# Two-layer recurrent block: ones on TensorE during the first loads, the next layer's input turned inside the first layer's tail

## The reference

```python
xn = layernorm(x)
s = L0_attention(xn)     # 32 heads of 16, 8 key/value heads, softmax, output projection Wo
g = silu(L0_ffn(xn))     # Hadamard transforms, up and gate products (2048), Hadamard transform, down product
x = x + s * g
xn = layernorm(x)
s = L1_attention(xn)     # q, k, v through a causal convolution of 4 taps and SiLU; gated delta rule over
                         # 6 heads of 64; RMS norm, gate, output projection
g = silu(L1_ffn(xn))     # sign(up) and sign(down) weights, ReLU between them
x = x + s * g
```

## Time and profile before

| | us |
|---|---|
| median of 3 runs | 1447.39 (1447.01 to 1448.87) |
| profiled execution | 1447.84 |
| its span | 1445.1 |
| TensorE busy | 1352.4 |
| VectorE busy | 1074.3 |
| ScalarE busy | 722.7 |
| GpSimd busy | 519.0 |
| second layer's block starts | 741.74 |

### The profile page before, as it was taken

The page is one execution under the profiler, slowest core; times in us unless marked ns, Lnnn a source line. Parts: engine busy times, 40 slices in busy tenths (PEclk is TensorE's granted clock), DMA queues, the critical chain, the costliest instruction groups (busy, mean ns, idle before and its releaser), DMA issues. The chain is left out here.

```text
span 1445.1 us, 24309 instructions
## 1 busy us (share of the span) xinstructions
PE 1352.4 (94%) x8972; PEld 663.8 (46%) x8972; DVE 1074.3 (74%) x1874; ACT 722.7 (50%) x1277; POOL 519.0 (36%) x434
## 2 busy tenths in 40 slices
PE   5988999999999999999889999998999899998998
PEld 2332333333333333333345458554675447654485
DVE  7889887787778787888728668578677796676745
ACT  5675665556656665566555513554235332354221
POOL 3599750122102220122116522274313543155331
PEclk9999999999999999999999999999999999999989
DMA  6420000000010000102530240001400113102211
GB/s 240 158 81 3 7 8 14 28 27 4 9 34 19 14 8 22 31 13 88 206 147 6 51 88 17 30 23 34 88 23 23 46 26 73 38 8 57 40 20 44
DMA packets 79573, 68.51 MB, mean 47 GB/s; under 512 B 45952, under 2 KB 67168, under 8 KB 76896
## 3 DMA queue, kind: packets, MB, share of 16 engines
q1 hardware_dynamic: 79456, 66.96, 15.6%
HBM read 44.87 MB, written 17.87 MB: 43 GB/s over the span
## 5 line engine op out<-in xcount | busy, mean ns | idle before, releaser
L610 DVE TENSOR_REDUCE mS<-bank 128x1 f16<-128x512 f32 x512 | 328.9, 685 | 114.5 <-PE bank L1113 112.4
L925 ACT ACTIVATE probs<-bank 128x512 f16<-128x512 f32 x512 | 277.2, 595 | 163.4 <-PE bank L1120 163.1
L1167 PE MATMUL bank<-rows,both 128*128 128x512 f16 x1024 | 243.0, 380 | 0.4 <-DVE th L639 0.3
L425 POOL TENSOR_TENSOR h<-th,h 128x512 f16<-128x512 f32 x61 | 71.5, 1172 | 219.0 <-ACT h L896 219.0
L1167 PEld LDWEIGHTS bank<-rows,both 128*128 128x128 f16 x1024 | 91.3, 98 | 121.2 <-issue 15.5
L2094 PE MATMUL fbank<-rows,both 128*128 128x512 f16 x512 | 119.1, 387 | 4.7 <-ACT hid L1915 4.7
L2078 PE MATMUL abank<-rows,both 128*128 128x512 f16 (+1 forms) x480 | 114.0, 390 | 4.6 <-PEq L149 4.6
L1113 PE MATMUL bank<-qk 32*128 32x512 f16 x512 | 100.5, 387 | 15.7 <-DVE mS L610 6.5
L2110 PE MATMUL fbank<-both,hid 128*128 128x512 f16 x512 | 111.2, 379 | 0.0
L1120 PE MATMUL bank<-qv,qk 32*128 32x512 f16 x512 | 99.9, 387 | 0.0
L1181 PE MATMUL bank<-dn,h 128*128 128x512 f16 x256 | 98.7, 386 | 0.0
(11 more groups left out here) (326 smaller groups left out, 2675.4 us busy)
## 6 DMA issues: line engine op xcount, KB each, us to landing
h<-in_ug SPq DMA_DIRECT2D x8, 1024.0 KB, 5.1
lt_scratch<-big SPq DMA_DIRECT2D x16, 384.0 KB, 2.7
dn<-in_down SPq DMA_DIRECT2D x2, 2048.0 KB, 11.0
x_scratch<-th SPq DMA_DIRECT2D x16, 256.0 KB, 2.2
res<-x_scratch SPq DMA_DIRECT2D x16, 256.0 KB, 3.6
out_x<-res SPq DMA_DIRECT2D x16, 256.0 KB, 2.0
both<-in_w SPq DMA_DIRECT2D x2, 1548.0 KB, 10.3
t_scratch<-tok SPq DMA_DIRECT2D x8, 384.0 KB, 3.5
```

The lines of the kernel that those rows point to most:

```text
L425: pool.tensor_tensor(h16(ft, 1), row32, h16(ft, 0), ALU.subtract).then_inc(S["row_lo"], 1)
L610: v.tensor_reduce(mS[:, u % 2, qt, 32 * j + DH:32 * j + DH + 1], SA[n % 2][:, :], AX.X, ALU.max).then_inc(S["max_done"], 1)
L925: a.activation(probs[:, n % (2 * G), :], SB[n % 2][:, :], ACT.Exp, scale=float(DH) ** -0.5).then_inc(S["p_ready"], 1)
L1167: mm = pe.matmul(GB[n % 2][:, :], w[:, kt, col:col + P], xnb(b, kt), start=r == 0, stop=r == 2 * KT - 1)
```

## The change

- TensorE no longer begins with the wait for the constants. It waits for `allone` and multiplies it with itself `WARM = 22` times (f32, 128x128 by 128 columns) into the bank `OB`, which nothing reads; then it waits for the constants as before.
- The second output projection of each batch moves from step 19 to step 20 (`OUT_STEP`), and with it its gate, residual and store. The residual inputs get a list of their own, `XRES_STEP = (17, 20, 24, 25)`: the third and the fourth are asked for at steps 24 and 25, not 28 and 35.
- `turn_next` moves from behind the last step to step 20 of the tail, ahead of that step's output projection. ScalarE's four `next_evict` move to the same step, behind its third sign.
- After the last step TensorE runs `project_next`: the 24 matmuls of the second layer's first `ba` and `pre_tile(0)`, into the banks that `layer1` expects them in. For this the eight banks are allocated once for both layers. In `layer1`, batch 0, these two tiles are left out and only their semaphore is raised.

```diff
-OUT_STEP = (17, 19, 28, 35)
+NEXT_STEP = 20
+OUT_STEP = (17, 20, 28, 35)
+XRES_STEP = (17, 20, 24, 25)
...
+WARM = 22
...
+    W["vpair"] = ctx.enter_context(nc.psum_tensor("vpair", [P, 2, 512], F32))
+    W["banks"] = [W["vpair"][:, 0], W["vpair"][:, 1]] + [ctx.enter_context(nc.psum_tensor(f"bank{i}", [P, 512], F32))[:, :] for i in range(2, 8)]
...
-                if b >= 0 and m in OUT_STEP:
-                    tt = OUT_STEP.index(m)
+                if b >= 0 and m in XRES_STEP:
+                    tt = XRES_STEP.index(m)
...
                 if t - B * BSTEPS in SIGN_AT:
                     raw_sign(SIGN_AT.index(t - B * BSTEPS))
-            for kt in range(KT):
-                next_evict(kt)
+                if t - B * BSTEPS == NEXT_STEP:
+                    for kt in range(KT):
+                        next_evict(kt)
...
         def _(pe):
+            pe.wait_ge(S["init"], 1)
+            for n in range(WARM):
+                pe.matmul(OB[:, 0:P], allone[:, :], allone[:, :], start=True, stop=True)
             pe.wait_ge(S["const_in"], 32)
...
+            def project_next():
+                pe.wait_ge(S["t_w1l"], KT)
+                pe.wait_ge(S["t_took"], KT)
+                pe.wait_ge(S["o_free"], NU)
+                for i, w in enumerate((slice(4 * KW, NW1), slice(ORDER[0] * P, ORDER[0] * P + P))):
+                    n = 0
+                    for kt in range(KT):
+                        for x, y in ((0, 0), (0, 1), (1, 0)):
+                            mm = pe.matmul(bank[3 + i][0:w.stop - w.start, :], W["w1"][:, x, kt, w], W["xT"][:, kt, y, :],
+                                           start=n == 0, stop=n == 3 * KT - 1)
+                            n += 1
+                    mm.then_inc(S["t_turn"], 1)
+                pe.wait_ge(S["t_turn"], KT + 2)
...
+                if b == B and m == NEXT_STEP:
+                    turn_next()
                 if b and m in OUT_STEP:
                     project_o((b - 1) * TT + OUT_STEP.index(m))
-            turn_next()
+            project_next()
...
-                three(bk[0:2 * LH, :], lambda i, kt: w1[:, i, kt, 4 * KW:NW1], x_half).then_inc(S["a_full"], 1)
+                if b:
+                    three(bk[0:2 * LH, :], lambda i, kt: w1[:, i, kt, 4 * KW:NW1], x_half).then_inc(S["a_full"], 1)
+                else:
+                    pe.sem_inc(S["a_full"], 1)
...
-                pre_tile(0)
+                if b:
+                    pre_tile(0)
+                else:
+                    afill("pre", 0)
+                    pe.sem_inc(S["a_full"], 1)
```

More of the change, by code:

```diff
@@ L154, in sem @@
             return ctx.enter_context(nc.semaphore(name))
-        bank = [ctx.enter_context(nc.psum_tensor(f"bank{i}", [P, 512], F32)) for i in range(8)]
+        bank = W["banks"]
         SA, SB, OB, GB, MISC = bank[0:2], bank[2:4], bank[4], bank[5:7], bank[7]
@@ L1303, in sem @@
             return ctx.enter_context(nc.semaphore(name))
-        vpair = ctx.enter_context(nc.psum_tensor("vpair", [P, 2, 512], F32))
-        vbank = [vpair[:, 0], vpair[:, 1], ctx.enter_context(nc.psum_tensor("vbank2", [P, 512], F32))]
-        abank = [ctx.enter_context(nc.psum_tensor(f"abank{i}", [P, 512], F32)) for i in range(3)]
-        fbank = [ctx.enter_context(nc.psum_tensor(f"fbank{i}", [P, 512], F32)) for i in range(2)]
+        vpair, vbank, abank, fbank = W["vpair"], W["banks"][0:3], W["banks"][3:6], W["banks"][6:8]
         ident16, cmat, rowm, blocks, hsel, onec, expo = (W[n] for n in ("ident16", "cmat", "rowm", "blocks", "hsel", "onec", "expo"))
```

## The result

The changed kernel takes **1449.78 us** (median of 20 executions, 1444.72 to 1456.46), the kernel before 1446.32 (median of 20 beside them, 1441.42 to 1448.87): 1.0028 of the time, 95% interval 1.0016 to 1.0039. It is slower by 3.5 us, where 6.0 us less had been forecast, and it lies above the range. The profiled execution takes 1449.62 us with a span of 1447.8.

What follows compares the result with a forecast made beforehand. TensorE, busy 94% of 1445.1 us, was taken as the bound, with waits or slow stretches in the first 27 us and at the seam. Terms -0.2 + 0.9 - 2.0 - 4.7 = -6.0 gave 1441.4 us, range 1437.0 to 1444.6.

Steps and rivals of the forecast that it cites:

- Ones: Kernel start: 22 added products hide before the first transposes, but scores from 22 us still start slow; -0.2 us.
- D: Kernel start: ones' weight loads and products don't overlap and the clock stays low, delaying the start; 1449.1 us, chance 0.04.
- The projection a step later: Three batches inside the loop: TensorE's q projection waits 0.3 us more for VectorE's product each time; +0.9 us.
- End of the first layer: First layer's tail: earlier loads let last signs and tanh start 1.7 us earlier, last-input wait gone; -2.0 us.
- rival B: Seam between layers: loads hold it (-0.8) and the third tile runs slow throughout (-3.7); 1443.6 us, chance 0.15.
- First tiles: Second layer's start: third tile complete 6.9 us after the block starts instead of 11.6; -4.7 us.
- Rival C: Second layer's start: VectorE's convolutions set the pace, so held tiles buy nothing; 1446.1 us, chance 0.06.
- Rival A: Seam: clock stays high, third tile comes at 4.5 us instead of 6.9; 1439.0 us, chance 0.15.

Runs made afterwards that it cites:

- short loads: Changed kernel without ones and with step 19 in the middle, its sixth to eighth raw weight loads cut to an eighth: 1431.79 us, one execution.
- filling products: Changed kernel without ones at the start and with step 19 in the middle, plus 7 products of ones ahead of the held tiles: 1444.22 us, 0.9982 of before.

## Why the prediction was wrong

- **Ones, -0.2 us.** At its place the term was right, and so was each of its steps: done at 8.6, fast projections, a pause of 4.56 us, scores where they were, -0.1 us at 260. The scores behind the pause were slow as foretold: projections 1.07 us, then the transform at 22.50 takes 2.08, and with 12 products in the pause 1.12. The rule of the Trainium skill that the prediction cites (page TensorE: Matmul & The Clock Gate, section HAM oscillation), that a long wait returns the clock to half, agrees with this. What failed is the sentence "So they cost nothing": I counted TensorE's time and left out that 88 more instructions (44 products and their weight loads) move everything fetched behind them. The runs put that at 3.0 to 7.2 us. None of my rivals had it; D foretold 1449.1, near what was measured, for another reason, records that do not overlap; that is refuted by 7.62 us for 44, so its number is luck.
- **The projection a step later, +0.9 us.** It is 3.3. The 0.3 us for the product were measured as 0.24. The step that failed is that I looked only at where the projection arrives and not at what it left: at step 19 its 1 us lay in a wait for VectorE's maxima.
- **End of the first layer, -2.0 us.** -0.5, less than my bound of -0.8, and not shown to be the change's. The step that failed is that the last signs and the last tanh start 1.7 us earlier: they start no earlier, since the eighth load landed when it had landed before, although its issue moved. That is the part of rival B on the loads. The short loads show that these loads hold the end. The working has a slip, too: its 1.7 and 0.5 us add up to 2.2, not 2.0, and TensorE's work as listed ends near 735.9, not 736.9.
- **First tiles, -4.7 us.** -3.9, near the bound (-3.7) for a third tile that is slow throughout, and -4.1 to -4.6 in four other traces. The mechanism was right: TensorE's 24 new matmuls and the turn hid as said, its pause is 3.46 us where 3.5 had been forecast, and it starts low again. The granted clock is 0.68 over 745 to 750.
- **Sum.** -0.1 + 3.3 - 0.5 - 3.9 = -1.2 us. With the three steps of 1.3 us at the shifted fetches this is +2.7, and with the half clock behind two more long waits (2 x 5.5 x 7/23 = 3.3) +6.0; with the rates of the second and the third batch, 4/5 and 1/6, it would be +8.0. The measured +3.5 lies between the first two, which says no more than that the parts are large enough. The kernel without the ones and with step 19 in the middle takes 1440.39, within the forecast's own width and 1.0 us from 1441.4. That is partly luck: it gains 5.4 us where the prediction's two terms for the seam say 6.7, and the forecast started from a median of 1447.39 of three executions, the comparison from 1445.74. The seam is worth near 5 us, less than it was taken for, and the ones and step 20 took more than that back.

Rival C (held tiles buy nothing) fell: without them the seam keeps 0.6 of its 4.3 us. Rival A did not occur in any trace; with filling products a part of it did, 1.0 us.

## What to carry to other kernels

Before an instruction is moved, ask what its old place was hiding as well as what the new one costs: a projection that sat in a wait cost 1.1 us a batch when it was moved, not the 0.3 us that were visible. Before instructions are added "for nothing" in an unrolled kernel, remember that they shift the instruction fetches of all that follows; after such an edit compare the traces stage by stage, also where nothing was edited, and test with instructions of the same number and no work. And where loads and the last consumer stand in a chain, issuing a load earlier can gain nothing: here the DMA engines were full, and the last tanh came no earlier.

## What the hardware showed unexpectedly

- One instruction packet of 16 KB among data transfers went with 1.1 to 1.4 us of delay for the engine that waited for the last of them, in 16 of 19 cases.
- A wait of TensorE of 1.4 to 1.7 us ahead of 24 products of 64x64 was followed by half clock for some 14 us in 7 of 23 cases, one of 0.7 us or less in none of 25. At 5.5 us each this could make much of the scatter between executions of one kernel, whose times go with their mean granted clock (correlation -0.95 in 35 executions); that it is these stretches was not tested.
- 44 f32 records of one column at the start took 9.54 us, those of 128 columns 7.62, and the k projection behind them 1.86 us against 1.02: less work took longer.
